# A last norm with VectorE's statistics two blocks ahead, and an earlier, wider timetable for a projection's parts, in a sorted-attention and mixture-of-experts kernel

## The reference

```
q, k, v = heads(x @ Wq.T + bq), heads(x @ Wk.T + bk), heads(x @ Wv.T + bv)     # 16 heads of 16
z = concat(k.reshape(B, T, 256) @ Wproj.T, q.reshape(B, T, 256) @ Wproj.T)     # 16 projections
out_i = sum over keys j of max(0, 1 - |z_i - z_j| / bw_h) * v_j / T            # "bump" attention
```

## Time and profile before

| | us |
|---|---|
| median of 3 runs | 2308.65 |
| range of the 3 runs | 2304.75 to 2308.7 |
| profiled execution, its own time | 2307.02 |
| span of the profiled execution | 2305.6 |

### The profile page before, as it was taken

How to read it: one execution, slowest core, us unless ns; L and a number is a source line. 1 busy time by engine, 2 the same in 40 slices (tenths; PEclk the granted TensorE clock), 3 DMA queues, 4 the chain that set the end, 5 groups by cost and what they waited for, 6 DMA issues and landing times.

```text
span 2305.6 us, 30639 instructions
## 1 busy us (share of the span) xinstructions
PE 1995.1 (87%) x11794; PEld 728.3 (32%) x11794; DVE 1949.6 (85%) x2792; ACT 1932.7 (84%) x1284; POOL 976.5 (42%) x412
## 2 busy tenths in 40 slices
PE   6799889899779899986798999868999996899966
PEld 4333233233112222221122222212222223577732
DVE  4597997897999898999998999999989997644427
ACT  3697997998999999999999999999999996122214
POOL 1100100100317458453185395422773674377745
PEclk9899999999889999999999999989989997899988
DMA  6425244435120202131202021312120305599987
GB/s 234 158 92 184 93 155 137 148 121 197 60 110 12 98 29 85 42 122 55 92 21 96 21 97 37 122 57 83 33 85 21 106 3 137 161 248 231 215 241 259
DMA packets 182231, 259.27 MB, mean 112 GB/s; under 512 B 22472, under 2 KB 162376, under 8 KB 173896
## 3 DMA queue, kind: packets, MB, share of 16 engines
q1 hardware_dynamic: 167600, 237.83, 30.9%
q0 software_dynamic: 12288, 18.88, 4.4%
q10 hardware_dynamic: 2200, 0.60, 0.1%
HBM read 187.25 MB, written 70.03 MB: 112 GB/s over the span
## 4 chain that ended last, share of the span: by engine, by line
PE 31%; DVE 24%; ACT 19%; POOL 13%; DMA 6%; issue 6%; SPq 0%; DVEq 0%; POOLq 0%; ACTq 0%
ACT TB L1105 18%; PE ps L902 14%; DVE TB L1429 12%; POOL scr L1610 8%; PE ps L812 6%; PE ps L849 5%; DVE TB L1451 3%; DMA y_rows<-ZB 3%; DVE st L1161 2%; PE ps L857 2%; POOL y_rows L1718 1%; PE ps L833 1%; PE ps L796 1%; DVE TB L1427 1%; DMA TB<-h_rows,ZB 1%
## 5 line engine op out<-in xcount | busy, mean ns | idle before, releaser
L1105 ACT ACTIVATE TB<-ZB,nzk 128x2048 f32<-128x2048 f32 x932 | 1778.4, 2011 | 79.2 <-DMA ZB<-zq_rows 57.2
L902 PE MATMUL ps<-TB,V 128*32 128x512 f32 x8192 | 1099.1, 630 | 208.9 <-DVE TB L1429 197.5
L1429 DVE TENSOR_SCALAR TB<-TB 128x2048 f32<-128x2048 f32 x932 | 1109.1, 1220 | 26.2 <-ACT TB L1105 25.0
L1610 POOL TENSOR_TENSOR scr<-ebase,scr 128x256 f32<-128x256 f32 x12 | 518.7, 43226 | 0.0
L902 PEld LDWEIGHTS ps<-TB,V 128*32 128x32 f32 x8192 | 186.5, 111 | 869.5 <-DVE TB L1429 571.3
L849 PE MATMUL ps<-XF,wsgu 128*128 128x512 f32 x512 | 278.8, 638 | 0.0
L1580 POOL TENSOR_SCALAR ve<-mv 128x4 f32<-128x4 f32 x44 | 40.4, 918 | 515.7 <-DVE mv L1165 515.6
L1451 DVE SCALAR_TENSOR_TENSOR TB<-ZB,kz 128x2048 f32<-128x2048 f32 x92 | 217.2, 2361 | 6.6 <-PE ps L902 6.6
L1608 POOL TENSOR_TENSOR scr<-ebase,scr 128x4 f32<-128x4 f32 x12 | 50.2, 4185 | 345.0 <-DVE scr L1295 345.0
L1134 ACT ACTIVATE ZB<-ps 128x128 f32<-128x128 f32 x64 | 17.7, 277 | 169.8 <-PE ps L983 169.8
L1597 POOL TENSOR_SCALAR ve<-mv 128x4 f32<-128x4 f32 x12 | 24.3, 2022 | 272.5 <-DVE mv L1165 272.5
(11 more groups left out here) (194 smaller groups left out, 1707.5 us busy)
## 6 DMA issues: line engine op xcount, KB each, us to landing
ZB<-zq_rows SPq DMA_DIRECT2D x64, 1024.0 KB, 7.0
scr<-fused_w SPq DMA_DIRECT2D x48, 512.0 KB, 3.3
TB<-y_rows SPq DMA_DIRECT2D x24, 512.0 KB, 7.9
TB<-in_egu_w SPq DMA_DIRECT2D x44, 256.0 KB, 3.6
y_rows<-zero SPq DMA_DIRECT2D x20, 512.0 KB, 4.9
fused_w<-TB SPq DMA_DIRECT2D x4, 2048.0 KB, 13.7
XF<-in_x SPq DMA_DIRECT2D x24, 256.0 KB, 5.4
v_rows<-scr SPq DMA_DIRECT2D x24, 256.0 KB, 2.2
```

Source lines behind the costliest of these rows:

```text
L902: ins = pe.matmul(ps[k][32 * c:32 * c + 32, :], V[:, o:o + 32], tile(n)[:, 512 * c:512 * c + 512], start=(kb == 0), stop=(kb == KB - 1))
L1105: act.activation(tile(e), zrow(head), ACT.Abs, bias=nzk[b][:, kb * H + g:kb * H + g + 1], scale=1.0).then_inc(s_abs, 1)
L1429: dve.tensor_scalar(T, T, 1.0, 1.0, ALU.min, ALU.subtract).then_inc(s_bump, 1)
L1610: pool.tensor_tensor(E4[:, :, 0:64], view(ebase[:, 0:1], 0, [[0, 4], [0, 64]]), E4[:, :, 0:64], ALU.pow).then_inc(s_ex, 1)
```

## The change

The last norm's VectorE program makes the statistics of group n + 2, where it made those of group n + 1, ahead of the addition of x1 to group n. The shared result is added four groups ahead, where it was three. In the timetable of batch 0, z's pieces stand 9/4 slots apart, where they stood 2 apart, and the first stands 4 slots sooner; the last stands one slot sooner. VectorE's copies of z and zT, TensorE's zT and the store "zq" stand 3 slots later than before.

```diff
 def z_at(f, tt):
-    return front_at(f, 3) + 21 + 2 * tt
+    return front_at(f, 3) + 17 + 9 * tt // 4
...
         r = z_at(f, 15)
-        dv += [(r + 5, "z", f), (r + 10, "zT", f)]
-        pe += [(r + 6, ("zT", f))]
-        sy += [(r + 11, "zq", f)]
+        dv += [(r + 9, "z", f), (r + 14, "zT", f)]
+        pe += [(r + 10, ("zT", f))]
+        sy += [(r + 15, "zq", f)]
...
-            vector_sums(0, v)
+            for n in range(2):
+                vector_sums(n, v)
             for n in range(NG):
-                if 12 <= n + 3 < NG:
-                    dve.wait_ge(q_f[(n + 3) % NY], 32 * ((n + 3) // NY + 1))
-                    t = yt[(n + 3) % NY][0]
-                    dve.tensor_tensor(t, t, y_of(last, n - 9), ALU.add).then_inc(s_fs, 1)
-                if n + 1 < NG:
-                    vector_sums(n + 1, v)
+                if 12 <= n + 4 < NG:
+                    dve.wait_ge(q_f[(n + 4) % NY], 32 * ((n + 4) // NY + 1))
+                    t = yt[(n + 4) % NY][0]
+                    dve.tensor_tensor(t, t, y_of(last, n - 8), ALU.add).then_inc(s_fs, 1)
+                if n + 2 < NG:
+                    vector_sums(n + 2, v)
                 k, m = use["ys", n, 1]
                 dve.wait_ge(empty[k], m + 1)
```

## The result

| | before | after |
|---|---|---|
| median, same chip (10 runs each) | 2306.9 us | 2316.27 us |
| range of the runs | 2303.46 to 2311.7 | 2312.58 to 2319.69 |
| span of the profiled execution | 2305.6 | 2315.4 |

The ratio is 1.0044 with a 95% interval of 1.0033 to 1.0055: **the change makes the kernel 9.4 us slower**. The forecast was within 0.2%, at 2308.0; the measured time lies just outside the upper end of the range, 2316.

The account below looks back on a forecast made before the run. ScalarE's distances were taken as the bound, held in three batch 0 windows by TensorE's progress through z. 2307.0 - 7.8 (last norm) + 8.5 (beside batch 0) = 2307.7, given as 2308.0 us; range 2299 to 2316 for 8 in 10.

Parts of the forecast that it names:

- The last norm: Last norm: statistics two groups ahead make TensorE's 3.44 us a group the pace instead of 3.87; -7.8 us, bounds -5 and -9.
- Both covers: Last norm: SyncE's queue stays filled though group 8's loads issue 2.4 us later; group 15's loads land before VectorE wants them.
- held by its loads: Rival, chance 0.1: the last norm is held by its loads and gains 5 us instead of 7.8; about 2310.5 us.
- Beside batch 0: Batch 0: piece 3's weight load passes v's last stores on SyncE's queue, so VectorE waits; +8.5 us, ends -1.6 and +16.2.
- f = 1: First z window: store landed 178.5, TensorE idle 4.2 us, low clock 2.0; slot 67 starts +6.5 us later, ends +2.7, +8.6.
- f = 2: Second z window, to slot 173: idling and low clock cost 6.4 us in place of 8.2; -1.8, ends -6.1 and 0.
- f = 3: Third z window, to slot 258: 2.5 us idle, then 1.1 more, 0.2 for the clock; +3.8, ends +1.8 and +7.6.
- ScalarE waits 1.5 us there: From 572 us on: the planner moves 66 own tiles of batches 1 to 3 earlier; ScalarE's work unchanged, worth nothing.
- The store is no obstacle: Rival, chance 0.30, faster: v's store lands in 2.2 us without a clock drop; batch 0 gives -1.6 to +3, total 2298 to 2302.
- The clock falls at all three places: Rival, chance 0.24, slower: 5.0 us landing and about 3 us per low stretch; batch 0 costs +16.2, total 2315.4 us.

Follow-up runs that it names:

- after again: The changed kernel without an edit, timed and profiled once more: 2316.53 us against 2307.75 for the kernel before, ratio 1.0039.
- z only: The kernel before with the new timetable of z alone: 2325.31 us, ratio 1.0057 to the kernel before.
- own tiles of before: The changed kernel with the planner given z's and zT's former slots, so it picks the former own tiles: 2315.88 us, ratio 1.0021 to the kernel before.
- before a, b: The kernel before, unedited, profiled twice more: 2313.64 and 2313.4 us, one execution each.
- stores first: The changed kernel with piece 3's weight load one slot later, behind the store of v's first half: 2298.31 us, ratio 0.9951 to the kernel before.
- start later: The changed kernel with all of z's pieces one slot later, z's and zT's stages unmoved: 2304.32 us, ratio 0.9982 to the kernel before.
- norm only: The kernel before with the last norm's part of the change alone: 2305.71 us against 2309.08, ratio 0.9972.
- the three kernels without them: The changed kernel with piece 3's load one slot later (2298.31 us), a second staging buffer for v (2298.44), or all z pieces one slot later (2304.32).

## Why the prediction was wrong

The mechanism was right in its links, and the size of one term was not: the timetable's cost beside batch 0. It was put at +8.5 us; in the windows it measured 10.1 and 12.1, and timed alone +13.2 (8.3 to 17.8). Since it stood against -7.8 for the norm, an error of a few us in it was the whole net result.

**The last norm: right, -7.8 predicted.** The stretch shortened by 7.4 and 7.7 us in the two profiles, and the timed part alone is -6.5 (-3.4 by the medians). Step by step: TensorE's pace of 3.44 up to group 9 came as predicted. VectorE's full loop took 4.07 to 4.15 us by the timeline (3.99 predicted), its loop without the shared addition 2.85 (2.85). Statistics of 15 ended 61.8 us after the first L1006 (61.0 predicted), and from there to x1 of 15 it took 5.9 us (6.3). Both covers held: the only wait for a load is the 0.21 us ahead of L1556 above. The rival "held by its loads" is out.

**Beside batch 0: the failed step, +8.5 predicted.** By slot 258 the changed kernel is at +12.3 and +14.5, of which 2.2 and 2.4 us were there at slot 44, ahead of z's windows; the rest, 10.1 and 12.1 us, is made from there on. The kernel before is at 0, +4.5 and +4.5 at slot 258, and at 0, +5.1 and +2.6 at slot 44; between the means of the two kernels lie 10.4 us. In the time from slot 44 to slot 67, 126 to 173 and 215 to 258, each less the first profile of before:

| window | predicted | after | after again | z only | own tiles of before | before a, b |
|---|---|---|---|---|---|---|
| f = 1 | +6.5 [2.7, 8.6] | +4.1 | +5.9 | +5.8 | +6.5 | -1.7, -1.0 |
| f = 2 | -1.8 [-6.1, 0] | +0.3 | -1.7 | +0.5 | +0.4 | -0.3, +0.8 |
| f = 3 | +3.8 [1.8, 7.6] | +5.8 | +7.9 | +5.8 | +5.8 | +1.6, +1.9 |

The prediction stood on the first profile, so the rows are set against that one. Against the mean of the three profiles of before, the four kernels' means are +6.5, -0.3 and +5.2, some 11.3 in all: that f = 1 fits to the tenth is partly luck, and f = 2 and f = 3 were put too low by 1.5 and 1.4 us.

- f = 1 was right, within its spread of +4.1 to +6.5: the store landed in 4.2 us (4.0 taken), TensorE idled 4.54 us (4.2), slot 67 started at 219.05 (219 predicted), and the granted clock fell, as the windows of the changed kernel show beside "stores first", which has no stall there (window: length, PE busy, granted clock, DMA share, GB/s; changed kernel first):

```profile
170.00:183.00 13.00, 8.85 (x42) 1.00 0.49 158
183.00:190.00 7.00, 6.61 (x28) 0.76 0.02 6
...
348.00:355.00 7.00, 6.20 (x23) 0.53 0.08 32
513.00:520.00 7.00, 5.83 (x23) 0.76 0.39 131
```

```profile
183.00:190.00 7.00, 7.00 (x38) 1.00 0.29 95
```

- f = 3 was mis-sized, by 2 us in three of the four profiles with the stall and by 4 in one (there the weight load left 1.8 us later, at 507.64 against 505.85, with ScalarE level at slot 215, so TensorE was late before the stall). "Piece 0 at 500.1, two loads' issues and the store" left out that SyncE issues the load of V and a zero store between the two (the fence above): the store left 1.32 us behind the weight load and took 4.7 us to land. "2.5 idle, then 1.1 more" was 3.77 idle in one piece and 0.32 more, and with it came the low clock (0.76), for which I had charged 0.2 us: a part at 2.08 us for 1.23 and a step at 1.65 for 1.06 are 1.4.
- f = 2 and f = 3 missed a term. The working took "that of slot 165" (and of 250) on TensorE as the gate of ScalarE's slot 173 (258), as before. But the change's last part stands at +51 (the prediction's +50 is wrong by one), one slot sooner than the +52 of before, so the last slot that TensorE holds back is 172 (257), and the next one comes at ScalarE's own pace of 1.9 us. ScalarE starts slots 173 and 258 at 1.12 and 1.18 us after TensorE's end of tiles 165 and 250, against 0.07 and 0.13 before (from the timelines). The lags are 1.12 and 1.18 in every kernel with 17 + 9/4, and again 0.07 and 0.13 with "start later", which puts the last part back to +52. That is +1.05 us for each of the two windows.

By the Trainium skill, page "DMA: Bandwidth & Descriptors", section "Queues, rings and completion order", the store would stand behind just the one load in its rings. With the 436 GB/s of its section "Bandwidth", which that section calls a ceiling of the ports and not the rate of such a transfer, I had estimated a landing of 3.4 us. The measured 4.2, 4.1 and 4.7 us at the three places are above it, as the prediction chose.

**Behind slot 258: "ScalarE waits 1.5 us there" stayed nearly true.** It idled 4.3 us in the changed kernel, 2.0 to 4.3 in three profiles of before; 2.3 and 1.5 us of it were short waits for L902 that no profile of before has. But other kernels idled up to 11.4 us there, mostly in single waits for the shared network's matmul. The longest, in "stores first", with no stall of v's anywhere near:

```profile
810.86 1.94 PE L902 MATMUL ps<-TB,V 128*32 128x512 f32 x8 [3.62 <-DVE TB L1429]
...
815.58 0.60 ACT L1063 ACTIVATE XF<-ps 128x512 f32<-128x512 f32 x1 [6.02 <-PE ps L849]
```

TensorE idles 3.62 us, its next steps take 1.94 us instead of 1.06, and ScalarE waits 6 us for L849 behind them. The change does not set this: norm only, whose program is that of before up to the last norm, has a wait of 6.0 us too, and its stretch from slot 258 to 1023 is 8.0 us longer than in the first profile of before. What sets it was not tried. From tile 1023 to the first L1006 the changed kernel differs from before by +1.9 and -0.1 us, the others by -1.6 to +3.3.

**The starting point.** The sum was made against a profile whose execution took 2307.02 us, at the median of the timed runs (2306.9); the two later ones, at 2313.6 and 2313.4, are slow draws. Against the first profile the last x1 of the changed kernel stands at +9.8 and +9.3, which is the timed +9.4 and +8.8. Stage by stage, for the first profile of the changed kernel: 2.2 up to slot 44, 10.1 to slot 258, 3.0 to the last tile, 1.9 to the first L1006, and -7.4 in the norm. Besides the windows the forecast had no term for the 2.2, the 3.0 and the 1.9. The 1.9 is -0.1 in the second profile; the other two came again (2.4 and 2.6), but programs without the change there show as much (+2.6 and +5.1 at slot 44 in the later profiles of before; 8.0 behind slot 258 in norm only). So whether the change costs anything outside the windows stays open. The timed parts do not settle it: +13.2 for the timetable, +16.2 by the medians, where the windows hold 10.1 to 12.1.

**The rivals.** "The store is no obstacle" is refuted by the waits and by the three kernels without them. "The clock falls at all three places" gave 2315.4, close to the measured time, and is partly right: the clock did fall at all three (0.76, 0.53, 0.76). But its price was not reached: +16.2 in the windows, against 10.1 and 12.1. It had 0.24; the argument against it, that f = 3 idles in two short pieces, was the wrong one.

**A version that beats both** came out of it: the change, with piece 3's load one slot later (2298.31, and 2296.03 with the own tiles of before), about 11 us or 0.5% below before. By the ratio of norm only, about 6 of these are the norm's.

## What to carry to other kernels

On a queue that blocks on its own waits, moving a load earlier also moves its wait ahead of everything that it passes: list those transfers, and for each the engine that waits for its landing. One late store in each of three fronts was worth some 18 us at slot 258 here (+12.3 against -6.2), and one load a slot later, or one more buffer, took it away. Before a single profile becomes the base of a sum of small terms, take a second one of the same program, and set the own time of each beside the timed runs: this sum's terms of 2 to 8 us stood on a profile whose repeats end 6.5 us later.

## What the runs showed of the hardware

- An idle time of TensorE of 3.6 to 4.5 us was followed, at all four places shown, by TensorE work at about the time of the lower clock: steps of 1.93 us instead of 1.06, or a part of 2.08 instead of 1.23. After 4.54 and 3.77 us the first step ran at 1.43 and 1.07, and the part behind it was the slow one, so the clock fell a little behind the restart. A shorter idle time decides nothing by itself: 2.33 us at one place of one program was followed by full clock in one execution (1.00) and by the low one in another (0.51).
- A store of 256 KB lands 2.2 us after its issue when alone, and in 4.1 to 4.7 us at the changed kernel's three places, issued 0.4 to 1.3 us behind a 512 KB load.
- Profiles of one program differ by up to 6.6 us (0.3%) at the last x1, made of pieces of 1 to 5 us at many places of the ledger, and ScalarE's idle time behind slot 258 differs by up to 7.8 us where the programs are the same up to the last norm (2.0 in before, 9.8 in norm only).
